# A decoder layer on one core: the opening reordered on three engines, the second step's queries in another PSUM bank, and the single jobs of self-attention moved to other places

## The reference

```
q,k,v = per head, 16 heads of 64;  a = softmax(causal(q k^T / 8));  attn = (a v) @ w_o
cross: 16 heads of 8, each as two sub-heads of 4 against 154 context rows;
       (softmax(q1 k1) - lam * softmax(q2 k2)) v,  lam = exp(lq1.lk1) - exp(lq2.lk2) + 0.2
ffn:   quantised tokens and ternary weights, 128 -> 512, depthwise conv of 3, silu, 512 -> 128
ln:    (x - mean) / sqrt(var + 1e-5), no weights
```

## Time and profile before

| | |
|---|---|
| median of 3 runs | 309.7 us (309.25 to 309.91) |
| the profiled execution: its time, its span | 310.28 us, 308.4 us |
| mean granted TensorE clock | 0.994 of full |
| busy: PE, DVE, ACT, POOL | 284.1, 217.0, 194.8, 143.4 us |

### The profile page before, as it was taken

How to read it: one execution, slowest core, us unless ns; L and a number is a source line. 1 busy time by engine, 2 the same in 40 slices (tenths; PEclk the granted TensorE clock), 3 DMA queues, 4 the chain that set the end, 5 groups by cost and what they waited for, 6 DMA issues and landing times.

```text
span 308.4 us, 6619 instructions
## 1 busy us (share of the span) xinstructions
PE 284.1 (92%) x2446; PEld 180.0 (58%) x2446; DVE 217.0 (70%) x482; ACT 194.8 (63%) x484; POOL 143.4 (46%) x253
## 2 busy tenths in 40 slices
PE   0899699899999989989799999999999998999996
PEld 0567466556666659656466676544545453356764
DVE  3668867886667760677667755898888869556855
ACT  2487457667788770596777762368877676835343
POOL 3504568976547790585236540039236373100241
PEclk9999979999999999999999999999999999999999
DMA  7820000000000000000000000000000000000001
GB/s 276 286 116 3 0 1 3 2 2 0 2 3 0 3 2 0 2 3 0 2 0 2 3 4 0 0 2 0 2 0 1 2 1 0 3 0 2 0 26 45
DMA packets 4835, 6.17 MB, mean 20 GB/s; under 512 B 834, under 2 KB 3650, under 8 KB 4676
## 3 DMA queue, kind: packets, MB, share of 16 engines
q1 hardware_dynamic: 4228, 5.29, 4.8%
q10 hardware_dynamic: 576, 0.47, 0.5%
HBM read 5.23 MB, written 0.52 MB: 19 GB/s over the span
## 4 chain that ended last, share of the span: by engine, by line
PE 74%; DVE 14%; ACT 7%; issue 3%; DMA 1%; ACTq 0%; DVEq 0%
PE bank L735 65%; PE bank L808 6%; ACT pr L550 4%; DVE nmax L1399 3%; DVE qk L1444 3%; DMA x_sb<-in_x 1%; ACT pT L550 1%; PE bank L960 1%; DVE xn L1343 1%; DVE stats L1330 1%; PE bank L862 1%; DVE pT L1415 1%; PE bank L1045 1%; DVE onT L1364 0%; DVE qs L1379 0%
## 5 line engine op out<-in xcount | busy, mean ns | idle before, releaser
L650 ACT ACTIVATE pT<-bank 128x512 f32<-128x512 f32 (+1 forms) x80 | 44.6, 601 | 25.6 <-PE bank L735 25.2
L340 POOL TENSOR_SCALAR pr<-pr,pinv 128x256 f32<-128x256 f32 (+2 forms) x96 | 45.5, 490 | 29.3 <-DVE pinv L1407 29.2
L1444 DVE TENSOR_REDUCE qk<-bank 128x4 fp32r<-128x616 f32 x64 | 49.1, 795 | 13.6 <-PE bank L735 13.4
L550 ACT ACTIVATE pr<-bank,nmax 128x256 f32<-128x256 f32 (+2 forms) x96 | 44.4, 480 | 18.2 <-DVE nmax L1399 17.9
L735 PE MATMUL bank<-qs 64*128 64x256 f32 (+3 forms) x256 | 50.7, 479 | 4.1 <-ACT pr L550 3.7
L1399 DVE TENSOR_REDUCE nmax<-bank 128x2 f32<-128x512 f32 (+2 forms) x48 | 31.6, 687 | 15.2 <-PE bank L735 15.1
L735 PE MATMUL bank<-pT,v_sb 128*64 128x128 f32 (+2 forms) x320 | 38.4, 385 | 0.0
L340 POOL TENSOR_SCALAR pT<-pT,pinv 128x512 f32<-128x512 f32 x32 | 21.7, 692 | 24.5 <-DVE pinv L1407 24.5
L1415 DVE COPY pT<-bank 128x512 f32<-128x512 f32 (+1 forms) x32 | 30.4, 949 | 1.1 <-PE bank L808 1.1
L735 PEld LDWEIGHTS bank<-pT,v_sb 128*64 128x64 f32 x320 | 21.1, 136 | 14.1 <-issue 11.0
L735 PE MATMUL bank<-km,qk 64*128 64x308 f32 x128 | 27.7, 366 | 1.2 <-DVE qk L1444 1.1
(11 more groups left out here) (196 smaller groups left out, 577.1 us busy)
## 6 DMA issues: line engine op xcount, KB each, us to landing
pT<-in_wqk SPq DMA_DIRECT2D x1, 1024.0 KB, 6.1
cw_sb<-in_cw SPq DMA_DIRECT2D x1, 768.0 KB, 8.9
x_sb<-in_x SPq DMA_DIRECT2D x2, 256.0 KB, 5.5
pT<-in_wv SPq DMA_DIRECT2D x1, 512.0 KB, 7.1
wo_sb<-in_wo SPq DMA_DIRECT2D x1, 512.0 KB, 7.3
out<-x_sb SPq DMA_DIRECT2D x6, 64.0 KB, 1.6
onT<-in_consts ACTq DMA_DIRECT2D x1, 256.0 KB, 6.6
pT<-in_xwk SPq DMA_DIRECT2D x1, 256.0 KB, 7.3
```

What stands on the lines that cost most here:

```text
L340: nc.gpsimd.tensor_scalar(d, d, pinv[:, t, a:a + 1], 1.0, ALU.mult, ALU.mult).then_inc(norm_done, 1)
L550: nc.scalar.activation(prob[r][:, a, at:at + w], bank[:, SP[k % 2] + a, at:at + w], ACT.Exp, bias=nmax[:, t, a:a + 1], accum_out=psum[:, t ...
L650: nc.scalar.activation(px[rows, i, :], bank[rows, (ST0, ST1)[i % 2], :], ACT.Exp, scale=SD ** -0.5).then_inc(xexp_done, 1)
L1444: nc.vector.tensor_reduce(m, s_in, AX.X, ALU.max, negate=True).then_inc(round_done, 1)
```

## The change

Nothing of the mathematics changes. The orders do:

- Opening, VectorE: the copies of the cross values move ahead of `stacked_key_rows(3)`; the identity cast, the lambda products and the lambda pair leave the opening (they go to steps 2, 1 and 4). ScalarE's lambda exponential goes to step 3. GpSimd's `low(xwq_l)` goes behind step 0's `normalise`. TensorE waits for `wsum_done` ahead of `project(1, 0)` and no longer behind `turn(0, 0)`.
- The queries of step 1 are written to OB, as those of all later steps, and no longer to PT; `turn(0, 0)`, which writes PT, no longer waits for `q_done`.
- `quantise_weights` is cut in three parts: first pass at the end of step 2 (or 4), second behind `row_max(n, 2)` of step 3 (or 5), third at the end of that step.
- Step 9: `out_proj` stands behind `weighted(8)`; `residual` behind `invert_sums(9, 2)`.
- Statistics: two tiles behind `row_max(10, 2)`, two at the end of step 10, the spreads behind `row_max(11, 2)`. The inverse root is made on GpSimd by a seed and three Newton steps: seed and two steps at the end of step 11, the third behind `normalise(12, 0)`. ScalarE's square root of this batch is gone.
- The normalised tiles are made at the end of step 12 (two) and behind `row_max(13, 2)` (two). `turn_norm` stands in step 13, between the two halves of `weighted(12)`, and its copies follow in step 13.

The diff, cut to its core (left out: `inverse_root` now calls `root_seed` and `root_step`; counts of semaphores in later code; `tile_stats` and `spreads` moved up and used by the last stage in the same order as before):

```diff
@@ -327,8 +327,6 @@
                 low(wqk_l[:, p, :, :], wqk_sb[:, p, :, :], wqk_h[:, p, :, :], wqk_low)
-            pool.wait_ge(asplit_h, 3)
-            low(xwq_l[:, :, :], xwq_sb, xwq_h[:, :, :], asplit_l)
...
@@ -370,9 +368,41 @@
                 xs = x_sb[:, NT * b:NT * b + NT, :]
                 nc.gpsimd.tensor_tensor(xs, xs, _repeat(xbo_sb[:, :], NT), ALU.add).then_inc(xb_done, 1)
 
+            def root_seed(b, k):
+
+                v, y = std[:, NT * b:NT * b + NT], rstd[:, NT * b:NT * b + NT]
+                pool.wait_ge(var_ready, k)
+                link(nc.gpsimd.tensor_scalar(y.bitcast(I32), v.bitcast(I32), -0.5, ROOT_SEED, ALU.mult, ALU.add))
+                link(nc.gpsimd.tensor_scalar(nroot[:, 0, :], v, -0.5, None, ALU.mult))
+                settle()
+
+            def root_step(b, done=False):
+                y, half, step = rstd[:, NT * b:NT * b + NT], nroot[:, 0, :], nroot[:, 1, :]
+                link(nc.gpsimd.tensor_tensor(step, half, y, ALU.mult))
+                settle()
+                link(nc.gpsimd.tensor_tensor(step, step, y, ALU.mult))
+                settle()
+                link(nc.gpsimd.tensor_scalar(step, step, 1.5, None, ALU.add))
+                settle()
+                last = nc.gpsimd.tensor_tensor(y, step, y, ALU.mult)
+                if done:
+                    last.then_inc(root_done, 1)
+                else:
+                    link(last)
+                    settle()
+
             for n in range(STEPS):
                 for r in range(3):
                     normalise(n, r)
+                    if n == 12 and r == 0:
+                        root_step(0, True)
+                if n == 0:
+                    pool.wait_ge(asplit_h, 3)
+                    low(xwq_l[:, :, :], xwq_sb, xwq_h[:, :, :], asplit_l)
+                if n == 11:
+                    root_seed(0, 3)
+                    root_step(0)
+                    root_step(0)
                 if n < NG:
                     spread_keys(n)
                 if n in (6, 7):
...
@@ -526,7 +540,7 @@
                 act.wait_ge(q_ps, n + 1)
                 if n >= 1:
                     act.wait_ge(s_ps, 3 * n)
-                nc.scalar.activation(qs[:, 0, :], bank[:, OB if n >= 2 else PT if n else PJ0, :], ACT.Identity, scale=DH ** -0.5).then_inc(q_done, 1)
+                nc.scalar.activation(qs[:, 0, :], bank[:, OB if n else PJ0, :], ACT.Identity, scale=DH ** -0.5).then_inc(q_done, 1)
 
             def stacked_keys(g):
...
@@ -610,13 +624,14 @@
             stacked_keys(3)
             nc.scalar.copy(xwq_h[:, :, :], xwq_sb).then_inc(asplit_h, 1)
 
-            act.wait_ge(lam_ready, 1)
-            nc.scalar.activation(lam_e[:, :], lam_e[:, :], ACT.Exp).then_inc(lam_exp, 1)
             query(1)
 
             for n in range(1, STEPS):
                 if n >= 2:
                     copy_heads(n - 2)
+                if n == 3:
+                    act.wait_ge(lam_ready, 1)
+                    nc.scalar.activation(lam_e[:, :], lam_e[:, :], ACT.Exp).then_inc(lam_exp, 1)
                 exps(n, 0)
                 keep_last(n - 1, 0)
                 keep_last(n - 1, 1)
@@ -624,13 +639,11 @@
                 if n + 1 < STEPS:
                     query(n + 1)
                 exps(n, 1, (1,))
-                if n == 12:
+                exps(n, 2)
+                if n == 13:
                     turned_norm(0, 3, PJ0)
-                exps(n, 2)
                 if n + 1 == STEPS:
                     query_parts(0)
-                if n == 10:
-                    root_of_variance(0, 3)
             copy_heads(STEPS - 2)
             keep_last(STEPS - 1, 0)
             keep_last(STEPS - 1, 1)
@@ -751,7 +764,7 @@
                     pe.wait_ge(pt_act, 2 * n - 3)
                 if n >= 2 and w == 0:
                     pe.wait_ge(pt_act, 2 * n - 2)
-                at = PJ0 if w or n == 0 else PT if n == 1 else OB
+                at = PJ0 if w or n == 0 else OB
                 mm3(bank[:, at, :], wqk_h[:, p, w, :], wqk_l[:, p, w, :], xT_h[:, b, :],
                     xT_l[:, b, :]).then_inc((q_ps, k_ps)[w], 1)
 
@@ -784,8 +797,6 @@
                 pe.wait_ge(norm_done, EXPS[k + 1])
                 if r == 0 and n >= 1:
                     pe.wait_ge(pt_dve, 2 * n)
-                if r == 0 and n == 0:
-                    pe.wait_ge(q_done, 2)
                 if r == 1:
                     pe.wait_ge(pt_dve, 2 * n + 1)
                 if r == 2:
@@ -1147,11 +1158,11 @@
             mm(bank[:, OB, 0:2], ones_sq, wsum[:, :], True, True).then_inc(wsum_ps, 1)
             pe.wait_ge(k_act, 2 * NG)
             project(1, 1)
+            pe.wait_ge(wsum_done, 1)
+            project(1, 0)
             pe.wait_ge(v_dve, 8)
-            project(1, 0)
             pe.wait_ge(vx_done, 4)
             turn(0, 0)
-            pe.wait_ge(wsum_done, 1)
 
             for n in range(1, STEPS):
                 scores(n, 0)
@@ -1165,14 +1176,17 @@
                 else:
                     pe.wait_ge(pt_act, 2 * STEPS - 2)
                     stack_queries(0)
+                turn(n, 0)
+                if n == 13:
+                    weighted(n - 1, range(0, 2))
+                    pe.wait_ge(k_done, 15)
+                    turn_norm(0, 3, PJ0)
+                    weighted(n - 1, range(2, NT))
+                else:
+                    weighted(n - 1)
                 if n == 9:
                     for p in range(NPAIR):
                         out_proj(0, p)
-                if n == 12:
-                    pe.wait_ge(k_done, 14)
-                    turn_norm(0, 3, PJ0)
-                turn(n, 0)
-                weighted(n - 1)
 
 
...
@@ -1325,24 +1339,35 @@
                 dve.wait_ge(dchain, chain[0])
 
 
+            def tile_stats(ts):
+                for t in ts:
+                    link(nc.vector.bn_stats(stats[:, t, :], x_sb[:, t, :]))
+
+            def spreads(ts):
+                settle()
+                for t in ts:
+                    link(nc.vector.bn_aggr(mv[:, t, :], stats[:, t, :]))
+                settle()
+                k = slice(ts[0], ts[-1] + 1)
...
+
+            def centred(ts):
+                for t in ts:
+                    last = nc.vector.tensor_scalar(xn[:, t, :], x_sb[:, t, :], mv[:, t, 0:1], rstd[:, t:t + 1],
+                                                   ALU.subtract, ALU.mult)
+                    if t != ts[-1]:
+                        link(last)
+                return last
 
             def norm_apply(b, k):
                 dve.wait_ge(std_ready, k)
                 link(nc.vector.reciprocal(rstd[:, NT * b:NT * b + NT], std[:, NT * b:NT * b + NT]))
                 settle()
-                for t in range(NT * b, NT * b + NT):
...
@@ -1352,17 +1377,20 @@
             def low(dst, whole, high, done):
                 nc.vector.tensor_tensor(dst, whole, high.bitcast(F32), ALU.subtract).then_inc(done, 1)
 
-            def quantise_weights(k):
+            def quantise_weights(k, part):
 
                 w = (w1_sb[:, :], w2_sb)[k]
-                dve.wait_ge(wsum_done, 1)
-                if k == 0:
-                    link(nc.vector.reciprocal(wscale[:, :], wmean[:, :]))
-                    settle()
-                link(nc.vector.tensor_scalar(wq1, w, wscale[:, k:k + 1], ROUND, ALU.mult, ALU.add))
-                settle()
-                link(nc.vector.tensor_scalar(wq1, wq1, ROUND, 1.0, ALU.subtract, ALU.min))
-                settle()
+                if part == 0:
+                    dve.wait_ge(wsum_done, 1)
+                    if k == 0:
+                        link(nc.vector.reciprocal(wscale[:, :], wmean[:, :]))
+                        settle()
+                    link(nc.vector.tensor_scalar(wq1, w, wscale[:, k:k + 1], ROUND, ALU.mult, ALU.add))
+                    return
+                settle()
+                if part == 1:
+                    link(nc.vector.tensor_scalar(wq1, wq1, ROUND, 1.0, ALU.subtract, ALU.min))
+                    return
...
@@ -1490,11 +1518,6 @@
             stacked_key_rows(2)
             value_copy(7)
             invert_sums(0, 2)
-            stacked_key_rows(3)
-            nc.vector.tensor_copy(ident_r[:, :], con[:, C_ID:C_ID + P]).then_inc(cast, 1)
-            link(nc.vector.tensor_tensor(lam_prod[:, :, :], lam_sb[:, 0:2, :], lam_sb[:, 2:4, :], ALU.mult))
-            settle()
-            nc.vector.tensor_reduce(lam_e[:, :], lam_prod[:, :, :], AX.X, ALU.add).then_inc(lam_ready, 1)
             for b in range(B):
...
@@ -1503,40 +1526,69 @@
                 at = 2 * C + C * b
                 nc.vector.tensor_tensor(vr[:, b, :], bank[0:4 * REM, PT + 1, at:at + C],
...
                                     ALU.max).then_inc(wsum_done, 1)
             keys(1)
-            dve.wait_ge(lam_exp, 1)
-            link(nc.vector.tensor_tensor(lam_c[:, 1:2], lam_e[:, 0:1], lam_e[:, 1:2], ALU.subtract))
-            settle()
```

(53 more changed lines are left out.)

54 lines of the change are left out of this document (14 added, 40 removed).

## The result

| | before | after |
|---|---|---|
| median of the runs | 309.55 us (309.25 to 309.91, 4 runs) | 300.54 us (300.22 to 300.66, 4 runs) |
| profiled execution: its time, its span | 310.28, 308.4 us | 300.5, 298.3 us |
| mean granted clock | 0.994 | 0.999 |

The ratio is 0.9706, with an interval of 0.9689 to 0.9723: 9.0 us faster. I had forecast 299.2 (298.0 to 302.8). The sum of the parts, 10.9 us of the profiled execution, came out as 9.8.

What follows compares the result with a forecast made beforehand. TensorE's own work of 8.36 us bounds an undisturbed step, so only disturbed steps can gain. Terms of 1.27 + 0.46 + 1.71 + 1.76 + 1.52 + 2.68 + 1.50 = 10.9 led to a forecast of 299.2 us, range 298.0 to 302.8.

Steps and rivals of the forecast that it cites:

- all gaps hold: Main forecast: moved jobs fit the engines' idle gaps to within half a us, 298.0 to 300.2 us; chance 0.58.
- Opening, 1.27: End of the opening: step 1's scores begin at 35.95 instead of 37.22, gain 1.27 us, bounds 0.8 and 1.3.
- Lambda 0.46: Opening: the turned tiles' copy no longer waits behind the lambda pair on VectorE; gain 0.46 us, bounds 0 and 0.46.
- clock 1.71: After the opening, 39.14 to 42.56: half-speed clock no longer occurs; gain 1.71 us, bounds 0 and 1.71.
- Ternary weights, 1.76: Step 2's to step 4's query copy: one weight pass per VectorE gap removes the excess, gain 1.76 us.
- Step 9, 1.52: Ahead of the output projection: TensorE's wait for VectorE's copy of the keys goes; gain 1.52 us, bounds 1.2 and 1.52.
- rival 3: Cross-attention and after: time is given back to something running by its own clock; half the gain lost, 304.5; chance 0.07.
- steps 10 and 11: Normalisation: statistics split, root moved from ScalarE to GpSimd, so the excess over undisturbed pitches goes; gain 2.68 us, bounds 1.9 and 2.68.
- Turned tiles, 1.50: Pitch from 149.81 to 160.29: the wait for PJ0 goes, 0.6 for transposes stays; gain 1.5 us, bounds 1.0 and 1.5.
- Median against profiled execution: Whole kernel: median 0.6 us below the profiled execution gives 298.8; forecast set at 299.2 as other runs may have less low clock.
- rival 1: Steps 1 to 6, 11, 12: VectorE and GpSimd collide, pitches of 8.5 or more, 301.3 us; chance 0.18.
- rivals 2 and 4: Opening: clock falls anyway, 300.9 us, chance 0.14; or stays low for long, 312.5 us, slower than before, chance 0.02.

Runs made afterwards that it cites:

- filler: Kernel before plus eight matmuls whose results nobody reads, in TensorE's idle time at the end of the opening: 308.92 us against 309.51, ratio 0.998.
- the last experiment: Kernel after with both repairs, GpSimd's conv-weight work at the end of step 9 and VectorE's wait for its third weight pass removed: 299.67 us, ratio 0.9689.
- Opening alone: Kernel before plus only the opening's part of the change (orders, lambda out, step 1's queries in OB): 307.0 us against 309.58, ratio 0.9921.

## Why the prediction was right, and where it was off

The forecast (all gaps hold, each disturbed step falls back to TensorE's own work) is what happened. Point by point:

- **Opening, 1.27.** Step 1's scores began at 35.51 where I had expected 35.95. With the start of this execution 0.44 earlier (first query copy at 15.28 in place of 15.72), the gain is 37.22 - 35.51 - 0.44 = 1.27. That it is exact is partly luck: two errors of about 0.13 cancel. The new wait for `wsum_done` did cost something: `wmean` was ready at 33.80, `project(1, 0)` began at 33.86, and from the first to the last of the six matmuls of the keys and queries it is 1.37 where it was 1.26. Against that, the copy of the queries started 0.04 behind the end of the projections (34.82), where I had put 0.2. The bank is worth 0.85 in all, by the pitch of a single run.
- **Lambda 0.46 and clock 1.71.** Together 2.17, measured 2.16, but the split was off and the errors cancel: 0.63 and 1.53 in the profiled execution. A bracket counts the wait only from the end of the matmuls before it; from start to start the wait was 0.63 longer than without it, not 0.46. And I had taken half of the low stretch as the loss. About 0.1 of the difference can be seen: with filler the next projection starts 0.34 behind the last mask matmuls of the scores, in the kernel before 0.23, so that some of the time won is waited away. The rest is not traced.
- **Ternary weights, 1.76.** From step 2's query copy to step 4's is now 65.78 - 48.99 = 16.79: 1.69. The 0.07 that stay are the wait that the last experiment removed.
- **Step 9, 1.52 (bounds 1.2 and 1.52).** This step failed, below its lower bound: 1.03. I looked at what TensorE had waited for ahead of the projection (VectorE's keys), and not at what the projection itself had been hiding: GpSimd's round 0, late behind 3.75 us of products. I had named the conv weights under rival 3 as made in the loop, and put nothing for what stands behind them. The same omission is in **steps 10 and 11**, 2.68, measured 2.45, where the ScalarE wait had hidden 0.17 of it. The experiment that moved those products gave 0.70 back. The residual, which I had seen fit with 0.1 to spare, did not quite: the maximum behind it started 0.92 behind the scores, 0.07 late.
- **Turned tiles, 1.50.** Measured 1.37, within its bounds. What stays is 0.74, not 0.6: from the start of `weighted(12)` to the next scores it is 153.16 - 150.10 = 3.06, one step earlier 144.06 - 141.74 = 2.32. The transposes take 0.59 of the difference by the chain; the other 0.15 lies in the two halves of `weighted`, why is not shown.
- **Median against profiled execution.** I left 0.4 of the 0.6 for a low clock that other runs might have less of. The timed runs bear this out in part: the clock costs 1.06 us in two thirds of the executions before and in none of the nine after. But the profiled execution before (310.28) lies 0.4 above the median of the low-clock runs too (309.87), so that the clock explains only the other 0.3 of what lies between it and the median of all, 309.55. Opening alone gave 2.6 by medians, and 1.8 against the high-clock runs beside it (308.81), which is near the 1.27 + 0.63 of its waits.

Of the 1.1 us between the sum (10.9) and what the profiled execution showed (9.8), step 9 is 0.49, step 11 0.23, the turned tiles 0.13, the weights' wait 0.07; the tail from the last query copy to the end of the span is 140.1 in place of 139.7, and the time outside the span 2.2 in place of 1.9; against these stands 0.44 from the earlier start. The longer tail is in the last stores: from VectorE's last operation to the end of the span it is 2.6 in place of 2.3. My chances add up to 0.97 faster and 0.02 slower, not the 0.96 and 0.03 that I wrote.

The rivals: no collision of VectorE and GpSimd reached the path (rival 1). Its sign, a pitch of 8.5 or more in step 11, did come with the 8.60, but moving the conv products brought that pitch to 8.36, so it was not a collision. GpSimd's normalisation beside the passes took 2.01 and 2.12 where it takes 1.84 alone, with room behind it, and the second pass, which took 0.70 beside GpSimd, took 0.41 in the loose gap, where GpSimd stood idle. The clock stayed up in all nine runs (rivals 2 and 4). Cross-attention came earlier by the whole sum (rival 3); the stretch from the last query copy passed its mark of 139.7 by the 0.3 of the stores. By the Trainium skill, "ScalarE: Activation LUTs", section "What ACT_TABLE_LOAD costs", a switch is a load of 1283 ns and a drain of about 1380; the load is in the trace (1.28), but in the experiment with the root on ScalarE an operation follows each of two loads at once, and both together, with the root between them, cost 1.5 us on the path, not 5.3.

## What to carry to other kernels

Before a long piece of TensorE's work is moved, list what each other engine finishes beside it: the engine that released the wait you remove is only the first, and the next late one was hidden by the very thing you move. Read small gains from the pitch of one repeated instruction, step by step; here it resolves 0.05 us, while the start alone moved by 1.3 us between executions. Count what a wait costs from start to start against an undisturbed step, not by the idle time in front of one row (0.63 against 0.46 here). And count the price of a low clock from runs that have it and runs that don't, not as half of the stretch.

## What was not expected of the hardware

The low stretch is not fixed to a kernel. At the same order of work, two thirds of the executions of the kernel before had it and a third not, and in the profiles that have it it begins at 37.0 (opening as before), 38.4, 38.7, 39.1 (before) or 39.4 us. With the idle time filled ten of twelve runs went without it. In the kernel after, a wait of 0.29 did not bring it in nine runs, nor did 0.78 and 0.34 in the one run with the queries in PT; but with the opening as before, and its waits of 1.25, 0.39 and 0.47, it came in only one of five. What else decides is open.

Some executions had a mean clock of 0.978 or 0.983 and took 2 to 4 us longer: three of 12 with the output projection moved, one of 12 with the weights moved, one of six with the normalisation moved, two of 12 with filler, one of six with both repairs, and none of 51 of the kernel before or nine of the kernel after. No profiled execution was one of these, so where in the run the clock was low, and what these kernels have in common, stays open.
